# Rounding the quantised tokens and the attention's output on ScalarE in place of VectorE

## The chip, the cores and the metric

The kernel runs on one core of a Trainium2 chip. The metric is the device time of one execution in microseconds (us). The core has TensorE (PE in the profile, PEld for its weight loads), VectorE (DVE), ScalarE (ACT), GpSimd (POOL) and SyncE (SP), which issues the DMAs. Each engine runs its own instructions in order; between engines there are only semaphores.

## The reference, cut to what matters

A block of cross attention and a mixture-of-experts feed-forward; the change lies in the attention alone. There are 8 batches of 512 tokens with 512 channels, 16 heads of 32 channels, and 1601 context rows for each batch.

```python
def _qdq(x):
    s = jnp.maximum(jnp.max(jnp.abs(x), axis=-1, keepdims=True) / 127.0, 1e-08)
    return jnp.clip(jnp.round(x / s), -127.0, 127.0) * s
...
q = _qdq(x) @ _qdq(wq).T + bq            # x is the layer-normed input
kv = cond @ wkv.T + bkv
k, v = jnp.split(kv, 2, axis=-1)
...
attn = jax.nn.softmax(jnp.einsum('bnhd,bmhd->bhnm', q, k) * scale, axis=-1)
o = jnp.einsum('bhnm,bmhd->bnhd', attn, v).reshape(B, N, C)
out = _qdq(o) @ _qdq(wp).T + bp
```

Each `_qdq` of activations rounds to integers. The kernel rounds by adding the constant ROUND = 12582912 to x times 127/max (a float32 of that size has no fraction bits left), and subtracts it again afterwards.

## The kernel before

**Units and slots.** The attention is one long pass over 32 units (8 batches times 4 blocks of four heads). A unit is cut into 28 slots: four heads times 7 groups of key tiles (six groups of 256 keys, one of 65). In a slot `s` PE computes the scores (L493) of slot s into one of two PSUM buffers, ACT takes their exponential (L642) into one of four buffers `a_p`, DVE subtracts the bfloat16 half of it to get the low part `a_p_low` (L764), and PE multiplies both halves with the values (L604) three slots later. Between scores and values PE does a slice of the key and value projections of the next unit (L510, L526). In this text unit 17 is the one that begins at 953.2 us and unit 18 the one from 1002.0 us; "slot 8 of unit 17" counts from the unit's first slot. The pattern of work repeats every four units, a batch.

**The order of everything else.** A class `Plan` puts all other work into slots by tables of numbers (QUANT_SLOTS, OUT_SLOTS, ...). Every engine walks over all slots and, in a slot, first does the exponential (ACT) or the low part (DVE) and then what the plan has there, in the order in which the code lists it. Neither the plan nor its tables are touched by the change.

**The work around the change.** Tokens of a later batch: mean and variance, centring on ACT (L693), the maximum on DVE (L824), scales and the factor `a_q_mul` (L830 to L835), the rounding `q_round` (L838), and three slots later `q_ints` on ACT (L700), which subtracts ROUND, and the transpose on PE. The attention's output of the batch before: POOL normalises it (L905 to L912), DVE takes maxima and the factor `a_o_mul` (L854 to L858), `round` (L861), then `ints` on ACT (L721), transposes, the projection, and on POOL the residual (L950, L956). Each rounding is done four times for a batch, on a tile of 128 tokens by 512 channels, in place. So a batch in the middle of the pass has eight of them: in its second unit `round` in slots 0, 12 and 24 and `q_round` in slots 8 and 20; in its third unit `q_round` in slots 4 and 16 and `round` in slot 8.

**Key and value projections.** Their PSUM results are in banks `ps_p` that ACT reads first (L652, L660: the high parts) and DVE second (L770, L779: the low parts, after which the bank is free). The keys' parts are then stacked by twelve DMAs (L422) into `a_k_stack`, which the scores of the next unit read; the second half of the stack is first needed in slot 5.

```python
for b, m in plan.at("q_round", s):
    dve.tensor_scalar(t["xm"][:, m, :], t["xm"][:, m, :], t["q_mul"][:, m:m + 1], ROUND, ALU.mult,
                      ALU.add).then_inc(q_rounded, 1)
```

## Time and profile before

| | |
|---|---|
| median of 3 runs | 2186.44 us (2184.74 to 2188.13) |
| the profiled execution's own time | 2184.58 us |
| its span, first to last instruction | 2182.8 us |
| busy, share of the span | PE 84%, DVE 82%, ACT 62%, POOL 44% |
| attention's slots | from 135.7 us to about 1690 us |
| granted TensorE clock in them | 0.97 to 1.00 of full speed |

Busy time says how long an engine had an instruction running. The rows further down show, for stretches of one unit, how much of it each engine was busy, who waited for whom, and what stood in a row at some roundings.

### The profile page before, as it was taken

How to read it: one execution, taken by the hardware profiler on the slowest of the kernel's cores; microseconds unless marked ns; L12 is line 12 of the kernel's file. 1: busy time of each engine (PE TensorE's matmuls, PEld its weight loads, DVE VectorE, ACT ScalarE, POOL GpSimd, SP SyncE). 2: the span in 40 equal slices, each digit the busy share in tenths (PEclk: the TensorE clock that was granted, in tenths of full speed). 3: DMA queues.
4: the chain of work that ended last, by engine and by line, in shares of the span. 5: the costliest groups of instructions: out<-in, count | busy, mean ns of one | idle time of the engine just before them, and what ended most of it. 6: DMA issues, size and time to landing. Idle time of an engine off the chain costs nothing. (4 is left out here: it accounts for less than half of the span.)

```text
span 2182.8 us, 60639 instructions
## 1 busy us (share of the span) xinstructions
PE 1822.8 (84%) x24804; PEld 1263.3 (58%) x24804; DVE 1795.8 (82%) x2402; ACT 1346.1 (62%) x1944; POOL 970.5 (44%) x900
## 2 busy tenths in 40 slices
PE   1379998999989998999999898989996216999996
PEld 1247776666666666666666666667774102555553
DVE  4459989899999998999999999989988395666665
ACT  0347876777777777777777777778776332333332
POOL 0002553375256436534733653365334201676765
PEclk7679999999999999999999999999998557999998
DMA  2332331242233223313322332232221244566785
GB/s 87 94 87 51 88 109 34 82 111 80 65 93 104 77 77 92 101 48 89 105 80 65 100 92 75 75 96 78 56 58 32 92 146 138 177 199 220 244 265 169
DMA packets 152823, 225.40 MB, mean 103 GB/s; under 512 B 33861, under 2 KB 87109, under 8 KB 152545
## 3 DMA queue, kind: packets, MB, share of 16 engines
q1 hardware_dynamic: 130736, 166.89, 26.5%
q0 software_dynamic: 21808, 54.58, 8.1%
q8 instruction: 202, 3.31, 0.7%
q14 instruction: 77, 0.62, 0.1%
HBM read 131.37 MB, written 71.32 MB: 93 GB/s over the span
## 5 line engine op out<-in xcount | busy, mean ns | idle before, releaser
L764 DVE TENSOR_TENSOR a_p_low<-a_p 128x1024 f16<-128x1024 f32 (+1 forms) x896 | 1097.2, 1247 | 134.7 <-ACT a_p L642 125.7
L642 ACT ACTIVATE a_p<-ps_s 128x1024 f32<-128x1024 f32 (+1 forms) x896 | 862.1, 967 | 384.9 <-PE ps_s L493 377.5
L493 PE MATMUL ps_s<-a_q_stack,a_k_stack 96*128 96x512 f16 (+1 forms) x1664 | 515.9, 385 | 77.3 <-DMA a_k_stack<-a_k_parts 53.6
L604 PE MATMUL ps_o<-a_v,a_p 128*128 128x65 f16 (+1 forms) x6656 | 447.5, 194 | 19.6 <-ACT a_o_sums L668 9.5
L604 PE MATMUL ps_o<-a_v,a_p_low 128*128 128x65 f16 (+1 forms) x6656 | 447.7, 194 | 0.0
L526 PEld LDWEIGHTS ps_p<-wkv,a_ctx 128*128 128x128 f16 x4992 | 330.4, 99 | 165.7 <-DVE a_v L779 59.2
L526 PE MATMUL ps_p<-wkv,a_ctx 128*128 128x128 f16 x4992 | 379.3, 222 | 44.8 <-DVE a_v L779 44.5
L604 PEld LDWEIGHTS ps_o<-a_v,a_p 128*128 128x128 bf16 (+1 forms) x6656 | 352.1, 98 | 100.3 <-DVE a_p_low L764 24.5
L510 PE MATMUL ps_p<-a_ctx,wkv 128*128 128x384 f16 (+2 forms) x1536 | 349.1, 337 | 37.0 <-DVE a_ctx L402 34.3
L604 PEld LDWEIGHTS ps_o<-a_v,a_p_low 128*128 128x128 f16 (+1 forms) x6656 | 318.1, 98 | 0.0
L510 PEld LDWEIGHTS ps_p<-a_ctx,wkv 128*128 128x128 f16 x1536 | 148.4, 98 | 185.5 <-DVE a_ctx L402 31.0
L905 POOL TENSOR_TENSOR a_o_full<-a_o_sums 128x128 f32<-128x128 f32 x128 | 147.8, 1183 | 202.6 <-ACT a_o_sums L668 202.6
L402 POOL TENSOR_TENSOR a_ctx<-a_ctx_raw,a_ctx 128x384 f16<-128x384 f32 (+2 forms) x112 | 169.2, 1523 | 112.6 <-ACT a_ctx L678 111.9
L1740 PE MATMUL f_ph<-wi_parts,f_xt 128*128 x864 | 200.6, 382 | 4.0 <-DVE f_xt L1807 4.0
L909 POOL TENSOR_TENSOR a_o_full<-a_o_full,o_inv 128x128 f32<-128x128 f32 x128 | 129.6, 1041 | 84.6 <-DVE o_inv L786 83.9
L493 PEld LDWEIGHTS ps_s<-a_q_stack,a_k_stack 96*128 96x128 f16 (+1 forms) x1664 | 114.4, 100 | 83.4 <-issue 77.9
L956 POOL TENSOR_TENSOR a_o_full<-a_o_full,a_x_in 128x512 f32<-128x512 f32 x32 | 88.5, 2767 | 157.9 <-DVE a_o_full L865 157.9
L1681 POOL DMA_INDIRECT f_xs<-d_xr,slots x72 | 81.8, 1136 | 157.6 <-POOLq L48 84.7
L1740 PEld LDWEIGHTS f_ph<-wi_parts,f_xt 128*128 128x128 f16 x864 | 84.7, 98 | 107.9 <-issue 8.3
L1793 ACT ACTIVATE f_gate<-f_ph 128x256 f32<-128x256 f32 x72 | 27.7, 385 | 141.8 <-PE f_ph L1740 141.8
L950 POOL TENSOR_TENSOR a_x_in<-a_x_in,bp_row 128x512 f32<-128x512 f32 x32 | 53.9, 1684 | 132.8 <-DMA a_x_in<-in_x_dram 132.8
L936 POOL TENSOR_SCALAR a_q_nmean<-a_q_mv 128x4 f32<-128x4 f32 x8 | 5.7, 717 | 234.2 <-DVE a_q_rstd L791 234.2
(232 smaller groups left out, 2186.6 us busy)
## 6 DMA issues: line engine op xcount, KB each, us to landing
a_k_stack<-a_k_parts SPq DMA_DIRECT2D x384, 80.0 KB, 2.1
d_ys<-f_y SPq DMA_DIRECT2D x72, 256.0 KB
a_ctx_raw<-in_ctx_dram SPq DMA_DIRECT2D x64, 192.0 KB, 2.5
a_q_stack<-d_q_t SPq DMA_DIRECT2D x96, 128.0 KB, 3.5
a_xm<-in_x_dram SPq DMA_DIRECT2D x8, 1024.0 KB, 5.9
a_ctx_raw<-in_ctx_dram SPq DMA_DIRECT2D x32, 256.0 KB, 4.7
d_q_t<-a_q_parts SPq DMA_DIRECT2D x32, 256.0 KB, 2.7
d_q_full<-a_xm SPq DMA_DIRECT2D x32, 256.0 KB, 2.9
```

Source lines behind the costliest of these rows:

```text
L402: eng.tensor_tensor(t["ctx"][:, 1, c, a:e], t["ctx_raw"][p % NRAW][:, 0:e - a], t["ctx"][:, 0, c, a:e], ALU.subtract).then_inc(ctx_split, 1)
L493: mm = pe.matmul(t["ps_s"][s % 2][0:r, n * N:(n + 1) * N], t["k_stack"][v % 2][0:TERMS * DH, j, kt * P:kt * P + r], t["q_stack"][v % 2][0: ...
L510: mm = pe.matmul(bank(job)[:, 0:e - a], t["wkv"][:, w_part, c, c0:c0 + P], t["ctx"][:, x_part, c, a:e], start=(m == 0), stop=(m == TERMS * ...
L526: mm = pe.matmul(bank(job)[:, n * P:(n + 1) * P], t["ctx"][:, x_part, c, kt * P:(kt + 1) * P], t["wkv"][:, w_part, c, c0:c0 + P], start=(m ...
L604: mm = pe.matmul(t["ps_o"][:, q * VC:(q + 1) * VC], part[0:r, n * N + q * P:n * N + (q + 1) * P], val, start=(g == 0 and n == 0 and low == ...
L642: act.activation(t["p"][s % NP][0:r, 0:len(tiles) * N], t["ps_s"][s % 2][0:r, 0:len(tiles) * N], ACT.Exp, scale=float(DH) ** -0.5 / WSCALE ...
L764: dve.tensor_tensor(t["p_low"][s % NP][0:r, 0:n], full, high, ALU.subtract).then_inc(lows, 1)
L905: last = pool.tensor_tensor(heads[:, j], sums[:, j, :, 0:DH], sums[:, j, :, DH:2 * DH], ALU.add)
L909: last = pool.tensor_tensor(heads[:, j], heads[:, j], t["o_inv"][:, v, j, :, None].to_broadcast([P, QT, DH]), ALU.mult)
L956: pool.tensor_tensor(t["o_full"][b % 2][:, m, :], t["o_full"][b % 2][:, m, :], t["x_in"][i % 2][:, :], ALU.add).then_inc(x2_ready, 1)
L1681: pool.indirect_dma_start(out=xs[n % NX][:, :], out_offset=None, in_=t["xr"][:, :], in_offset=bass.IndirectOffsetOnAxis(ap=t["slots"][:, n ...
L1740: last = pe.matmul(ps_h[n % 2][:, :], xt[n % 2][:, x_part, c, :], t["wi"][:, bass.ds(e, 1), w_part, c, :].rearrange("p a f -> p (a f)"), s ...
```

## The change

Both roundings leave DVE and become activations on ACT: `Identity(scale * x + bias)`, with the factor as scale and a new tile `a_toround`, filled with ROUND, as bias. They stand in the same slots of the plan. In ACT's code `q_round` stands behind centring and ahead of `q_ints`, and `round` behind `q_high` and ahead of `ints`. ACT waits for the factors by `q_scaled`, which was there, and a new semaphore `scaled`. DVE has a wait on the earlier batch's roundings before it overwrites a factor.

```diff
+        scaled = sem("a_scaled")
...
+                for b, m in plan.at("q_round", s):
+                    act.wait_ge(q_scaled, 2 * b + 2)
+                    act.activation(t["xm"][:, m, :], t["xm"][:, m, :], ACT.Identity, bias=t["toround"][:, 0:1],
+                                   scale=t["q_mul"][:, m:m + 1]).then_inc(q_rounded, 1)
...
+                for b, m in plan.at("round", s):
+                    act.wait_ge(scaled, b + 1)
+                    act.activation(t["o_full"][b % 2][:, m, :], t["o_full"][b % 2][:, m, :], ACT.Identity,
+                                   bias=t["toround"][:, 0:1], scale=t["o_mul"][:, m:m + 1]).then_inc(rounded, 1)
...
+            dve.memset(t["toround"][:, :], ROUND)
...
+                    if b >= 1:
+                        dve.wait_ge(q_rounded, b * QT)
                     dve.tensor_tensor(t["q_mul"][:, :], t["tmp"][:, :], t["q_rstd"][:, :], ALU.mult).then_inc(q_scaled, 1)
                     dve.wait_ge(q_scaled, 2 * b + 2)
-                for b, m in plan.at("q_round", s):
-                    dve.tensor_scalar(t["xm"][:, m, :], t["xm"][:, m, :], t["q_mul"][:, m:m + 1], ROUND, ALU.mult,
-                                      ALU.add).then_inc(q_rounded, 1)
...
-                    done(dve.reciprocal(t["o_mul"][:, :], t["so"][:, :]))
-                for b, m in plan.at("round", s):
-                    o = t["o_full"][b % 2][:, m, :]
-                    dve.tensor_scalar(o, o, t["o_mul"][:, m:m + 1], ROUND, ALU.mult, ALU.add).then_inc(rounded, 1)
+                    if b >= 1:
+                        dve.wait_ge(rounded, b * QT)
+                    dve.reciprocal(t["o_mul"][:, :], t["so"][:, :]).then_inc(scaled, 1)
+                    dve.wait_ge(scaled, b + 1)
```

The order of DVE's instructions in unit 17, from the factor `a_q_mul` on (slot 6 to slot 13), before:

```order
L835 TENSOR_TENSOR a_q_mul<-a_tmp,a_q_rstd 128x4
L764 TENSOR_TENSOR a_p_low<-a_p 128x1024 x2
L838 TENSOR_SCALAR a_xm<-a_xm,a_q_mul 128x512
L764 TENSOR_TENSOR a_p_low<-a_p 128x1024
L779 TENSOR_TENSOR a_v<-ps_p,a_v 128x16x32
L764 TENSOR_TENSOR a_p_low<-a_p 128x1024 x2
L865 SCALAR_TENSOR_TENSOR a_o_full<-ps_p,a_so,sp_row 128x512
L764 TENSOR_TENSOR a_p_low<-a_p 128x1024
L770 SCALAR_TENSOR_TENSOR a_k_parts<-ps_p,bk,a_k_parts 128x384
L861 TENSOR_SCALAR a_o_full<-a_o_full,a_o_mul 128x512
L764 TENSOR_TENSOR a_p_low<-a_p 65x512
```

And the same place of DVE in the changed kernel, whose line numbers are some nine higher (L773 is L764, L788 is L779, L779 is L770):

```order
L847 TENSOR_TENSOR a_q_mul<-a_tmp,a_q_rstd 128x4
L773 TENSOR_TENSOR a_p_low<-a_p 128x1024 x3
L788 TENSOR_TENSOR a_v<-ps_p,a_v 128x16x32
L773 TENSOR_TENSOR a_p_low<-a_p 128x1024 x2
L874 SCALAR_TENSOR_TENSOR a_o_full<-ps_p,a_so,sp_row 128x512
L773 TENSOR_TENSOR a_p_low<-a_p 128x1024
L779 SCALAR_TENSOR_TENSOR a_k_parts<-ps_p,bk,a_k_parts 128x384
L773 TENSOR_TENSOR a_p_low<-a_p 65x512
```

The two roundings are gone from between the low parts; nothing else has moved on DVE.

ACT's order at the same place (slot 6 to slot 12 of unit 17), before:

```order
L642 ACTIVATE a_p<-ps_s 65x512
L642 ACTIVATE a_p<-ps_s 128x1024
L729 COPY a_oq_t<-ps_p 128x512
L642 ACTIVATE a_p<-ps_s 128x1024 x2
L660 CAST a_v<-ps_p 128x16x32
L668 COPY a_o_sums<-ps_o 128x260
L642 ACTIVATE a_p<-ps_s 128x1024 x2
L700 ACTIVATE a_xq<-a_xm,a_unround 128x512
L642 ACTIVATE a_p<-ps_s 128x1024
L652 ACTIVATE a_k_parts<-ps_p,bk 128x384
```

And in the changed kernel (L643 is the exponential, L661 and L653 the high parts of values and keys):

```order
L643 ACTIVATE a_p<-ps_s 65x512
L643 ACTIVATE a_p<-ps_s 128x1024
L738 COPY a_oq_t<-ps_p 128x512
L643 ACTIVATE a_p<-ps_s 128x1024
L698 ACTIVATE a_xm<-a_xm,a_toround,a_q_mul 128x512
L643 ACTIVATE a_p<-ps_s 128x1024
L661 CAST a_v<-ps_p 128x16x32
L669 COPY a_o_sums<-ps_o 128x260
L643 ACTIVATE a_p<-ps_s 128x1024 x2
L705 ACTIVATE a_xq<-a_xm,a_unround 128x512
L643 ACTIVATE a_p<-ps_s 128x1024
L653 ACTIVATE a_k_parts<-ps_p,bk 128x384
```

A rounding (L698) now stands between two exponentials, and the later exponentials, high parts and copies are behind it; `round` of slot 12 (L723) follows right behind the last row.

## Rows read from the trace of the kernel before

**Rows 1.** The page: busy times, and VectorE's busy tenths in 40 slices.

```profile
PE 1822.8 (84%) x24804; PEld 1263.3 (58%) x24804; DVE 1795.8 (82%) x2402; ACT 1346.1 (62%) x1944; POOL 970.5 (44%) x900
...
DVE  4459989899999998999999999989988395666665
```

**Rows 2.** Windows of units 17 to 19: length; busy us (instructions) of each engine; clock; DMA.

```profile
953.20:1002.00 48.80, 44.65 (x697) 32.66 (x696) 47.51 (x56) 36.61 (x51) 16.57 (x14) 1.00 0.24 59
1002.00:1052.90 50.90, 45.28 (x701) 32.97 (x700) 46.62 (x46) 38.34 (x57) 28.95 (x19) 1.00 0.33 91
1052.90:1103.50 50.60, 46.35 (x701) 34.00 (x700) 45.20 (x54) 38.84 (x56) 35.76 (x32) 0.97 0.38 110
```

**Rows 3.** Waits in units 16 to 19: us in total, times, longest.

```profile
ACT a_p L642 <- PE ps_s L493: 45.8, 55, 4.7
...
DVE a_p_low L764 <- ACT a_p L642: 13.4, 17, 2.0
...
PE ps_s L493 <- DMA a_k_stack<-a_k_parts: 8.6, 4, 3.4
PE ps_p L526 <- DVE a_v L779: 7.6, 5, 2.4
...
PE ps_s L493 <- ACT a_p L642: 0.3, 1, 0.3
```

**Rows 4.** VectorE's groups by form, units 4 to 30 (311.4 to 1641.5 us).

```profile
L764 DVE TENSOR_TENSOR a_p_low<-a_p 128x1024 f16<-128x1024 f32 x648 | 851.0, 1332 | 101.4 <-ACT a_p L642 95.5
...
L861 DVE TENSOR_SCALAR a_o_full<-a_o_full,a_o_mul 128x512 f32<-128x512 f32 x28 | 30.5, 1091 | 0.0
...
L838 DVE TENSOR_SCALAR a_xm<-a_xm,a_q_mul 128x512 f32<-128x512 f32 x24 | 18.1, 754 | 0.0
```

**Rows 5.** One rounding line alone, same stretch: ns min/median/max.

```profile
L861 DVE TENSOR_SCALAR a_o_full<-a_o_full,a_o_mul x28: 469/1234/1499, 360.6 to 1613.7; 128x512 f32<-128x512 f32 x28
```

**Rows 6.** One of ScalarE's groups by form in the same stretch.

```profile
L742 ACT ACTIVATE a_xn_parts<-a_o_full,a_rstd 128x512 f16<-128x512 f32 x24 | 17.5, 731 | 0.0
```

**Rows 7.** Timeline of VectorE, slots 8 and 9 of unit 17.

```profile
972.66 0.47 DVE L838 TENSOR_SCALAR a_xm<-a_xm,a_q_mul 128x512 f32<-128x512 f32 x1
973.06 1.21 DVE L764 TENSOR_TENSOR a_p_low<-a_p 128x1024 f16<-128x1024 f32 x1
974.19 0.68 DVE L779 TENSOR_TENSOR a_v<-ps_p,a_v 128x512 f16<-128x512 f32 x1
```

**Rows 8.** Timeline of TensorE: the stalls behind rows 7 and rows 9.

```profile
974.93 0.34 PE L526 MATMUL ps_p<-wkv,a_ctx 128*128 128x128 f16 x3 [1.68 <-DVE a_v L779]
```
```profile
1024.55 0.34 PE L526 MATMUL ps_p<-wkv,a_ctx 128*128 128x128 f16 x3 [2.36 <-DVE a_v L779]
```

**Rows 9.** Timeline of VectorE, slots 8 and 9 of unit 18.

```profile
1020.19 1.50 DVE L861 TENSOR_SCALAR a_o_full<-a_o_full,a_o_mul 128x512 f32<-128x512 f32 x1
1021.61 2.28 DVE L764 TENSOR_TENSOR a_p_low<-a_p 128x1024 f16<-128x1024 f32 x1
1023.81 0.68 DVE L779 TENSOR_TENSOR a_v<-ps_p,a_v 128x512 f16<-128x512 f32 x1
```

**Rows 10.** Timeline of GpSimd at the same place.

```profile
1019.14 2.26 POOL L950 TENSOR_TENSOR a_x_in<-a_x_in,bp_row 128x512 f32<-128x512 f32 x1
1021.37 1.44 POOL L956 TENSOR_TENSOR a_o_full<-a_o_full,a_x_in 128x512 f32<-128x512 f32 x1
```

**Rows 11.** Timeline of VectorE, then of ScalarE, slots 20 and 21 of unit 17.

```profile
990.93 0.47 DVE L838 TENSOR_SCALAR a_xm<-a_xm,a_q_mul 128x512 f32<-128x512 f32 x1
991.32 1.21 DVE L764 TENSOR_TENSOR a_p_low<-a_p 128x1024 f16<-128x1024 f32 x1
```
```profile
990.06 1.02 ACT L642 ACTIVATE a_p<-ps_s 128x1024 f32<-128x1024 f32 x1 [0.17 <-PE ps_s L493]
```

**Rows 12.** Timeline of VectorE, slots 24 and 25 of unit 17.

```profile
998.12 1.50 DVE L861 TENSOR_SCALAR a_o_full<-a_o_full,a_o_mul 128x512 f32<-128x512 f32 x1
999.53 1.21 DVE L764 TENSOR_TENSOR a_p_low<-a_p 128x1024 f16<-128x1024 f32 x1
```

More of the change, by code:

```diff
@@ L981, in attention @@
         t["sx_row"], t["unround"] = sb("sx_row", [P, N]), sb("unround", [P, 1])
+        t["toround"] = sb("toround", [P, 1])
         t["st"], t["q_mv"] = sb("st", [P, 2 * QT, 6]), sb("q_mv", [P, QT, 2])
```

## The prediction

> **What bounds the kernel now.** The page comes first. DVE and PE are each busy over four fifths of the span, and in the attention DVE stands at 8 to 9 tenths in nearly every slice [rows 1]. Two engines near full say little until one sees which waits for which, so I next cut one batch into its four units [rows 2]. In unit 17 DVE is busy 47.5 of 48.8 us: nothing is left to take out but DVE's own work. PE is busy 44.7 there and 45.3 of 50.9 in unit 18. So PE stands idle 4.1 us in unit 17 (48.80 − 44.65) and 5.6 in unit 18 (50.90 − 45.28), and ACT 12 in each. Third, the waits of these four units [rows 3]: PE waits 7.6 us in five waits for the values' low part on DVE, and 8.6 us in four waits for the stacked keys, once in each unit; the DMAs of that stack start when DVE has written the keys' low part. PE waits only 0.3 us for ACT's exponential, and ACT 45.8 us for PE's scores. So the pace is set by two queues in turn: PE, while nothing is missing, and DVE at the few places in a unit where a bank or the key stack is late. ACT has spare time and is ahead of DVE at most places, but not at all: DVE waits 13.4 us in 17 waits for it.
>
> **What is removed.** 64 roundings leave DVE: 52 in units 4 to 30 [rows 4], four in units 1 and 2, four before the first slot, four after the last. Their busy time in units 4 to 30 is 30.5 + 18.1 = 48.6 us. That is no gain yet, for two reasons.
>
> First, a rounding alone takes 0.47 us, and 0.40 of queue time, since the next one starts 0.40 after it (973.06 − 972.66) [rows 7]. The rest of the long ones is waiting: L861 goes from 469 to 1499 ns with a median of 1234 [rows 5]. In rows 9 the one at 1020.19 takes 1.50 us while POOL works at L950 until 1021.40 [rows 10]; the low part after it takes 2.28 in place of 1.21 [rows 7, 9] while POOL works at L956. DVE's and POOL's instructions take turns. If the rounding goes, POOL's work is still there, and the next low part meets it instead. So I hold 0.40 of each as surely freed, and the rest as put off to the next low part. The Trainium skill says the same in its own terms (SBUF — State Buffer, section "SBUF: two separate sides": VectorE and GpSimd share a port pair that one of them holds for a whole instruction while the other blocks, also where a VectorE operation has two SBUF inputs); by that rule alone each of the 52 is worth 0.40, 20.8 us in all at most, and the 48.6 us would not come out.
>
> Second, a freed microsecond counts only where PE waits for DVE next. So I go through the eight roundings of a batch:
>
> - Slot 8 of unit 17: two instructions behind the rounding stands the values' low part (L779 at 974.19), for which PE stalls 1.68 us [rows 7, 8]. All of the 0.40 comes out. Gain 0.4 (bounds 0 and 0.4).
> - Slot 8 of unit 18: the same form, stall 2.36 us [rows 8]. The low part at 1021.61 can start up to 1.42 earlier (1021.61 − 1020.19) [rows 9]. It then waits out L950 in the rounding's place, and L956 meets a low part that stands behind L779, when PE has already been released. What is put off is put off past the stall. Gain 1.4 (bounds 0.4 and 1.42).
> - Slot 24 of unit 17: behind it stand a low part and the keys' low part L770, from which the key stack starts [rows 12]. The rounding held 1.41 (999.53 − 998.12), but the exponential now comes later too and POOL's turn stays. I take 0.3, near the low bound (bounds 0 and 1.4).
> - Slots 0 and 12 of unit 17 and slots 4, 16 and 20: slot 0 lies ahead of the unit's wait for the key stack in slot 5, which absorbs it; the others have no PE stall for DVE close behind. At slot 20 I see a loss of lead: the exponential ends at 991.08 (990.06 + 1.02) and DVE wants it at 990.93 [rows 11]; moved back by a rounding it ends near 991.7, and the low part starts 0.4 later than its 991.32 in place of earlier. The five together 0.1 (bounds −0.4, which is slot 20 alone, and 2.0 = 5 × 0.40).
>
> Sum of a batch: 0.4 + 1.4 + 0.3 + 0.1 = 2.2 us. Six batches have all eight roundings: 13.2 us. The four roundings in units 1 and 2 and the four in units 29 and 30 count as half a batch each, 2.2 us together. Sum 15.4 us.
>
> **What is added.** On ACT 64 activations of 128 × 512 with a factor and a bias. The nearest rows are ACT's own of that size, in SBUF, with one such operand: 0.73 us each [rows 6]. No row has both operands as tiles; I take 0.73, with 0.7 and 1.0 as bounds (the upper one is the duration of an exponential on twice the columns [rows 11]). ScalarE: Activation LUTs, section "What ACT_TABLE_LOAD costs", of the Trainium skill has each pointer operand at about 93 ns more; that would be 0.82, and 0.09 × 52 = 5 us of ACT's time. On the path I cost the activations at nothing in the sum: ACT is idle 12 us in each of the two units [rows 2] and gets 5 × 0.65 = 3.3 us (0.73 less the usual overlap of 0.08) in the one and 2.0 in the other. If that cover fails, it is the last rival below. Queued behind a rounding on ACT are the next exponential, the high parts and the copy of the output sums. At slot 8 of unit 17 ACT may also wait for `a_q_mul`, about 1 us, because DVE runs some two slots behind; for the same reason nobody is waiting for the exponentials then. The new waits on DVE (on roundings of the batch before) were met a batch ago: nothing. The memset is one of 128 × 1 ahead of the loop: nothing. The start and the end, eight roundings outside the slots, cost 0.73 in place of 0.47: at most 8 × 0.26 = 2 us if all lie in the chain; against it the last two no longer stand behind other work on DVE. I take nothing.
>
> **The sum.** The profiled execution took 2184.58 us, 1.86 below the median of the runs. 2184.58 − 15.4 = 2169.2; beside the median, 2186.44 − 15.4 = 2171.0. A measurement of this kernel tells 0.2%, or 4.4 us, from no change.
>
> **The rivals.**
>
> *The long roundings' whole time comes out.* For it: over half of them are long [rows 5], and PE's stalls, 4.1 + 5.6 = 9.7 us in two units, have room for it. Against it: the turns with POOL. DVE would lose 48.6 + about 2.6 in units 1 and 2, less 0.08 of overlap for each of 56 and less the seven of slot 4 (some 0.6 each), after which DVE waits anyway: 42.5 us. Time: 2186.4 − 42.5 = 2144; with three quarters of it delivered 2155. Chance 0.12.
>
> *No change that counts.* PE's own work plus the key stack set the pace. For it: PE at 44.7 to 46.4 us in all four units [rows 2], stack waits of 8.6 us in each batch [rows 3] for which twelve DMAs, not DVE, are the long part; what DVE wins it spends waiting for exponentials. Against it: the 7.6 us for L779. Time: 2186 (2182 to 2190). Chance 0.17.
>
> *Slower: the exponentials come late.* A rounding in ACT's queue moves the following exponential by 0.65 us. It decides where ACT's lead over DVE is less than 0.65; from the starts in the trace it is less at slots 20 and 24 of unit 17 and slots 4 and 8 of unit 18, more at the other four. If the lead were gone everywhere, which it may be once DVE has less to do, all 52 would cost 0.65 less the 0.40 freed: +13 us, 2199. The Trainium skill speaks for this side (ScalarE: Activation LUTs, "Rules for kernel authors": adds and multiplies belong on VectorE); the rows agree so far that 0.73 stands against 0.47 [rows 6, 7]. Chance 0.16.
>
> *My forecast*, 0.55: 2171, its own range 2163 to 2182 (the four places at their low bounds give 0.4 us a batch, 2184; with each long one at its full price about 2163).
>
> **How the numbers follow.** Faster: 0.50 of my case and 0.12 of the first rival, 0.62. Within 0.2%: 0.05 and 0.17, 0.22. Slower: 0.16. The range leaves out the far half of the first rival and most of the last: 2155 to 2190.
>
> **What the profile after would show.** DVE's busy time down by 48 to 55 us if its contention goes with the roundings, by 30 if it moves to L764 (now 1332 ns on average for the large form in units 4 to 30). ACT's up by 64 × 0.73 = 47 us. The waits of PE for L779 shorter, above all the one in slot 11 of a batch's third unit (now 2.36 us); PE's waits for ACT still small. Unit 17 near 48.1 and unit 18 near 49.1 us. I am wrong if DVE waits for exponentials by more than it lost in work (then slower), if the low parts do not get longer and the units lose 6 us a batch (then 2150), or if the stack waits grow by what L779's lose (no change).

## The result, and the profile after

The changed kernel took 2149.9 us (median of four runs, 2142.85 to 2151.05) against 2185.59 for the kernel before on the same chip (four runs, 2179.82 to 2188.13): ratio 0.9834, interval 0.9805 to 0.9863, a gain of 36 us. The forecast was 2171, a gain of 15.4; the time lies below the range. The profiled execution took 2150.41 us, 34.2 less than the one of before (2184.58).

The page of the changed kernel, busy times and VectorE's tenths (as [rows 1]):

```profile
PE 1807.6 (84%) x24745; PEld 1258.3 (59%) x24804; DVE 1770.9 (82%) x2339; ACT 1385.7 (64%) x2008; POOL 996.7 (46%) x900
...
DVE  4469989899999899999989999999997395676665
```

DVE is as full as before. Its busy time fell by 24.9 us, where the two lines of the roundings alone held 48.6 in units 4 to 30 [rows 4].

The windows of units 17 to 19 after (as [rows 2]; columns length, PE, PEld, DVE, ACT, POOL, clock, DMA):

```profile
937.00:985.20 48.20, 44.70 (x697) 32.75 (x698) 45.36 (x52) 39.58 (x56) 16.23 (x14) 1.00 0.23 59
985.20:1033.60 48.40, 44.85 (x698) 33.19 (x700) 44.97 (x43) 40.25 (x60) 31.83 (x21) 1.00 0.35 98
1033.60:1080.60 47.00, 44.44 (x699) 32.93 (x700) 44.76 (x54) 38.91 (x56) 40.64 (x30) 1.00 0.39 115
```

Unit 17 is 0.6 us shorter, unit 18 2.5 and unit 19 3.6. Unit 19 has no rounding in it and was in no term of the sum. Its clock rose from 0.97 to 1.00. Keep these two facts.

The waits of units 16 to 19 after (as [rows 3]: us in total, times, longest):

```profile
ACT a_p L643 <- PE ps_s L494: 34.6, 46, 3.1
...
DVE a_p_low L773 <- ACT a_p L643: 11.3, 17, 2.0
...
PE ps_p L527 <- DVE a_v L788: 5.2, 4, 1.9
...
PE ps_s L494 <- DMA a_k_stack<-a_k_parts: 4.9, 4, 1.7
...
PE ps_o L605 <- ACT a_o_sums L669: 2.3, 4, 1.0
```

PE's wait for the values' low part fell from 7.6 to 5.2 us, and that for the stacked keys, to which the prediction gave 0.3 us a batch, from 8.6 to 4.9. DVE doesn't wait longer for exponentials (13.4 and 11.3). PE waits a little longer for ScalarE: 2.3 us for the copies of the output sums, 1.2 before.

**Where the 34.2 us lie.** The first exponential starts at 135.7 us before and at 132.9 after (2.8); the slots take 1544.6 and 1514.3 us (30.2, of which units 4 to 27, the six batches that are alike, 28.4: 1189.9 and 1161.5); what follows, 1.1. I added up PE's idle stretches of over 0.12 us in units 4 to 27 from the records. They are 106.6 us before and 87.4 after: 19.2 of the 28.4. The other 9.2 lie in the time between the stalls, of which 34.1 us are at half of PE's clock before and 17.1 after (below). The places, as means over the six batches (a place is the slot by ScalarE's exponentials; a stall can fall one slot earlier than the slot whose scores wait):

```
place of PE's stall                   before  after
third unit, slot 11 (L779)              2.36   0.95
fourth unit, slot 4 (key stack)         3.07   1.69
third unit, slots 22 and 24 (for DVE)   0.80   0.00
second unit, slot 11 (L779)             1.68   0.99
second unit, slot 4 (key stack)         1.19   0.72
third unit, slot 4 (key stack)          1.77   1.43
third unit, slot 17 (ACT's copy)        0.31   1.01
second unit, slot 3 (DVE's low part)    0.00   0.58
```

### The profile page after: what moved, and what is told of

It is laid out like the page before. It is cut to its first block and busy times, and to the rows that moved or that the text cites. A ratio compares the mean times of both kernels' runs of the same rounds, so it can differ in the third digit from the quotient of the medians.

```text
span 2148.7 us, 60597 instructions
## 1 busy us (share of the span) xinstructions
PE 1807.6 (84%) x24745; PEld 1258.3 (59%) x24804; DVE 1770.9 (82%) x2339; ACT 1385.7 (64%) x2008; POOL 996.7 (46%) x900
## 5 line engine op out<-in xcount | busy, mean ns | idle before, releaser
L773 DVE TENSOR_TENSOR a_p_low<-a_p 128x1024 f16<-128x1024 f32 (+1 forms) x896 | 1120.8, 1274 | 125.7 <-ACT a_p L643 117.5
L643 ACT ACTIVATE a_p<-ps_s 128x1024 f32<-128x1024 f32 (+1 forms) x896 | 861.3, 966 | 309.1 <-PE ps_s L494 303.0
L527 PEld LDWEIGHTS ps_p<-wkv,a_ctx 128*128 128x128 f16 x4992 | 325.3, 98 | 144.9 <-DVE a_v L788 39.8
L527 PE MATMUL ps_p<-wkv,a_ctx 128*128 128x128 f16 x4992 | 373.2, 220 | 28.6 <-DVE a_v L788 28.4
L511 PE MATMUL ps_p<-a_ctx,wkv 128*128 128x384 f16 (+2 forms) x1536 | 346.6, 335 | 34.2 <-DVE a_ctx L403 34.1
L914 POOL TENSOR_TENSOR a_o_full<-a_o_sums 128x128 f32<-128x128 f32 x128 | 157.3, 1257 | 201.7 <-ACT a_o_sums L669 201.7
L403 POOL TENSOR_TENSOR a_ctx<-a_ctx_raw,a_ctx 128x384 f16<-128x384 f32 (+2 forms) x112 | 196.6, 1773 | 83.8 <-ACT a_ctx L679 83.6
L918 POOL TENSOR_TENSOR a_o_full<-a_o_full,o_inv 128x128 f32<-128x128 f32 x128 | 120.5, 970 | 80.8 <-DVE o_inv L795 80.1
L965 POOL TENSOR_TENSOR a_o_full<-a_o_full,a_x_in 128x512 f32<-128x512 f32 x32 | 77.7, 2430 | 132.5 <-DVE a_o_full L874 132.5
```

The costliest lines, as they stand in the source:

```text
L403: eng.tensor_tensor(t["ctx"][:, 1, c, a:e], t["ctx_raw"][p % NRAW][:, 0:e - a], t["ctx"][:, 0, c, a:e], ALU.subtract).then_inc(ctx_split, 1)
L511: mm = pe.matmul(bank(job)[:, 0:e - a], t["wkv"][:, w_part, c, c0:c0 + P], t["ctx"][:, x_part, c, a:e], start=(m == 0), stop=(m == TERMS * ...
L527: mm = pe.matmul(bank(job)[:, n * P:(n + 1) * P], t["ctx"][:, x_part, c, kt * P:(kt + 1) * P], t["wkv"][:, w_part, c, c0:c0 + P], start=(m ...
L643: act.activation(t["p"][s % NP][0:r, 0:len(tiles) * N], t["ps_s"][s % 2][0:r, 0:len(tiles) * N], ACT.Exp, scale=float(DH) ** -0.5 / WSCALE ...
L773: dve.tensor_tensor(t["p_low"][s % NP][0:r, 0:n], full, high, ALU.subtract).then_inc(lows, 1)
L914: last = pool.tensor_tensor(heads[:, j], sums[:, j, :, 0:DH], sums[:, j, :, DH:2 * DH], ALU.add)
```

## The experiments

Ratios are to the kernel before, measured beside each kernel on the same chip, with the 95% interval. On two of the chips the last stage after the attention takes 539 to 554 us in place of about 500, and the kernel before 2230 to 2238 us in all; so I compare ratios, and of the traces only units 4 to 27. All of these kernels have the same plan as before unless the diff says otherwise; each was profiled once. The diffs are cut: "..." and the text say what is left out. What each was for: which roundings carry the gain; whether it is DVE's freed time or another order of turns; what ScalarE's added work costs; and whether the key stack, through the queues behind it, is the second half of the gain.

### Only the tokens, only the outputs, and one of the outputs

Three kernels from the one before. `e1_tokens_only` moves `q_round` alone to ScalarE, `e2_outputs_only` moves `round` alone, and `e3_fourth_output_only` only the `round` of the last 128 tokens, slot 8 of a batch's third unit (e3's lines, first ScalarE's, then VectorE's):

```diff
+                for b, m in plan.at("round", s):
+                    if m < 3:
+                        continue
+                    act.wait_ge(scaled, b + 1)
+                    act.activation(t["o_full"][b % 2][:, m, :], t["o_full"][b % 2][:, m, :], ACT.Identity,
+                                   bias=t["toround"][:, 0:1], scale=t["o_mul"][:, m:m + 1]).then_inc(rounded, 1)
...
                 for b, m in plan.at("round", s):
+                    if m == 3:
+                        continue
...
```

> Only the rounding of the tokens is on ScalarE; the outputs' stays on VectorE. Theory A (a rounding is worth its own 0.40 us of VectorE's queue where TensorE stalls behind it; what it waited for GpSimd moves to the next low part): the stall of 1.7 us in slot 11 of a batch's second unit shrinks to 1.0 to 1.3, that in slot 11 of the third unit stays at 2.4, and the waits for the key stack shrink by under 1 us a batch; 7 to 12 us faster, 2174 to 2179. Theory B (the whole duration comes out, in proportion: 18.1 of 48.6 us): 13 us faster, 2172, and VectorE's low parts do not get longer. If ScalarE's load hurts on its own, no gain.

> Only the rounding of the attention's output is on ScalarE. Theory A: the stall in slot 11 of the third unit goes from 2.4 to 1.0 us, that of the second unit stays at 1.7 or gets shorter by the 0.4 of slot 0 at most, the waits for the key stack shrink by 1 to 2 us a batch; 18 to 26 us faster, 2160 to 2168. Theory B: 30.5 of 48.6 us in proportion, 22 us faster. The two halves together should give the 35.7 us of the change if the effects add; less if they share the same stalls.

> Only one of the eight roundings of a batch moves, the fourth tile of the output, in slot 8 of a batch's third unit, two instructions ahead of the values' low part. Theory A: the stall of 2.4 us in slot 11 of that unit goes to about 1.0, nothing is lost on ScalarE; 1.4 us times 7 is 10 us, 2176, and more only if the key stack's wait in the next unit shrinks too (then up to 17). Theory B: an eighth to a sixth of the change's gain, 5 us, 2181.

Measured: e1 2204.3 us, 0.9883 (0.9866 to 0.9901); e2 2206.92, 0.9906 (0.9889 to 0.9922); e3 2209.02, 0.9912 (0.9885 to 0.9939), with 2229.56 before. e1 gained 25 us where 7 to 12 were expected. By the ratios the two halves make 48 us together, more than the change's 36; by the traces units 4 to 27 are 9.8 us shorter in e1 and 18.1 in e2, together 27.9 where the change has 28.4. Slot 8 of the third unit is what takes slot 11's stall from 2.36 to 0.95: it is 0.96 in e2 and 1.01 in e3, but 2.14 in e1. The stall in slot 4 of the fourth unit goes the other way: 1.30 in e1, 2.76 in e2, 3.12 in e3. So that one is the tokens' doing. The new stall of slot 3 in the second unit is in e2 (0.48) and not in e1, that of slot 17 in the third in e1 (1.01) and not in e2.

### DVE's load given back, ScalarE's doubled

`e8_dve_too` is the changed kernel with a rounding of a tile that nobody needs left on DVE at each of the old places; `e7_act_twice` is the changed kernel with each rounding activation done once more into a tile that nobody reads.

```diff
 e8
+                for _ in plan.at("q_round", s):
...
+                    dve.tensor_scalar(t["dummy"][:, :], t["bv_row"][:, :], t["bv_row"][:, 0:1], ROUND, ALU.mult,
+                                      ALU.add).then_inc(dummied, 1)
...
 e7
+                    act.activation(t["dummy"][:, :], t["xm"][:, m, :], ACT.Identity, bias=t["toround"][:, 0:1],
+                                   scale=t["q_mul"][:, m:m + 1])
...
```

> The changed kernel, with a rounding of idle data into an idle tile put back on VectorE in the places of the old ones (it leaves nothing out and adds 64 operations). VectorE has its old load, ScalarE the new one. If the gain is VectorE's time alone and ScalarE's load is free: 2186, as before. If the late exponentials cost: 2190 to 2199. If the gain came from elsewhere: below 2180.

> The changed kernel with each rounding activation done twice, the first into an idle tile: ScalarE gets another 0.8 us at each of the 64 places. If ScalarE's load is free, as the gain suggests: as the changed kernel, ratio 0.983. If the new waits for the copied sums (slots 3 and 17) grow with it: 0.6 us more at two or three places of a batch, 8 to 13 us slower than the changed kernel, ratio 0.988 to 0.990. Late exponentials everywhere would give 1.00.

Measured: e8 2213.34 us, 0.9927 (0.9909 to 0.9944); e7 2213.43, 0.9911 (0.9892 to 0.9929). With DVE's work given back the stall of slot 11 is 2.36 again, so that part is DVE's time. Yet 0.7% stay, and the fourth unit's stall stays at 1.77. DVE has as many instructions there as before; only their operands and their starts differ. So the load alone doesn't make that part. ScalarE's share is not free: twice the activations take back about half of the gain by the ratios (0.9834 to 0.9911, from different chips), and 6.2 of the 28.4 us by the traces (units 4 to 27: 1161.5 to 1167.7).

### Clearing the queue in front of the key stack, without moving a rounding

The stack's second half is put into SP's queue behind context loads, which wait for a buffer that GpSimd frees, and a store, which waits for GpSimd's addition L956. `e10_before_five_buffers` gives the context loads a fifth buffer; `e12_before_queue_clear` also puts the store four slots later.

```diff
-NRAW = 4
+NRAW = 5
...
-    "gate": dict(logits=1), "project": dict(y=1, x2=2, x2_store=8), "turn": dict(turned=1, project=4),
+    "gate": dict(logits=1), "project": dict(y=1, x2=2, x2_store=12), "turn": dict(turned=1, project=4),
```

> The kernel before with five buffers for raw context instead of four; nothing else. Theory C (the key stack of a batch's fourth unit is late because the queue of SP stands at a context load that waits for a buffer, which GpSimd frees late, since its addition L956 takes 6.66 us there in place of 2.2): the stack's DMAs start right behind the keys' low part, the stall in slot 4 of the fourth unit goes from 3.1 us to 1.2 to 1.7, and the kernel gets 8 to 15 us faster with no work moved at all. If the lateness is VectorE's own, nothing changes.

> The kernel before with five buffers for raw context and the store of the residual sum four slots later, behind the key stack's DMAs in SP's queue. With five buffers alone the queue stood at that store instead, which waits for the same slow addition L956. Theory C: nothing in the queue waits for L956 ahead of the stack now, so the stall of slot 4 in the fourth unit goes from 3.1 to about 1.3 us although L956 still takes 6.66 us; 10 to 20 us faster than before. If the stack is late for another reason: stall near 2.9 and at most 10 us.

Measured: e10 2226.7 us, 0.9954 (0.9935 to 0.9972); e12 2170.8, 0.9929 (0.9903 to 0.9955). From the keys' low part to the stack's first DMA it takes 4.4 us before, 3.05 in e10 and 2.57 in e12, and the stall goes from 3.07 to 2.87 and 2.36. L956 stays at 6.66 us in both. That is far less than the 1.2 to 1.7 and about 1.3 expected, and the shorter stall bought nothing there: units 4 to 27 take 1189.1 and 1188.8 us, against 1189.9 before, with 47.8 and 41.0 us at half clock in place of 34.1. Most of what the two kernels gained lies elsewhere: by their traces 3.5 and 3.3 us before the first exponential and 4.7 and 4.2 in the slots outside units 4 to 27. Nor is the queue clear: in the batch shown further down the stack's DMAs of e12 stand behind a context load that is issued at 1052.70 us, as GpSimd's second conversion ends.

### The stack put earlier

`f1_before_stack_early` puts the stack's last part one slot behind the keys' in place of three, ahead of the loads and the store.

```diff
-                self.put("stack", job[1], job[2] - 2, s + 3)
+                self.put("stack", job[1], job[2] - 2, s + (1 if job[2] == 3 else 3))
```

> The kernel before with the second half of the key stack two slots earlier in SP's order, ahead of the context loads of those slots; what it waits for (the keys' low part) is unchanged. In the kernel before its first DMA starts 4.4 us behind that low part in a batch's fourth unit, with five buffers 3.0, with both queue edits 2.6, and the stall of slot 4 went 3.1, 2.9, 2.4. Theory C: the DMA now starts at once (0.03 us) in all units, the stall is 1.0 to 1.4 us and L956 may stay at 6.66 us; 8 to 14 us faster. If the stall stays above 2.3 although the DMA starts at once, the lateness is elsewhere.

Measured: 2193.21 us against 2187.56, 1.0033 (1.0017 to 1.0049): slower, where 8 to 14 us faster were expected. The stack's first DMA is still 2.57 us behind the keys' low part and not 0.03, again with context loads ahead of it that wait for a conversion on GpSimd. The stall is counted in slot 3 now, with 2.31 us, and ScalarE waits for the context. Its row in the waits of f1, units 4 to 30, then that of the kernel before:

```profile
ACT a_ctx L678 <- DMA a_ctx_raw<-in_ctx_dram: 34.3, 11, 6.1
```
```profile
ACT a_ctx L678 <- DMA a_ctx_raw<-in_ctx_dram: 0.6, 2, 0.4
```

Who stands behind in SP's queue is only exchanged. No run takes the lateness of GpSimd's conversions out of the queue altogether, so how much of the stall they make isn't shown by an edit of the queue.

### Only the first head of the stack waited for

`e5_before_first_head` (and `e6_after_first_head`, the same edit on the changed kernel) lets slot 5 wait for the first head's three DMAs alone, and slot 12 for the other nine.

```diff
                 if s % SLOTS == LATE_GROUP:
-                    pe.wait_ge(keys_in[1][v % 2], 16 * TERMS * HB * (v // 2 + 1))
+                    pe.wait_ge(first_in[v % 2], 16 * TERMS * (v // 2 + 1))
+                if s % SLOTS == GROUPS + LATE_GROUP:
+                    pe.wait_ge(keys_in[1][v % 2], 16 * TERMS * (HB - 1) * (v // 2 + 1))
...
```

> The kernel before; TensorE's wait in slot 5 of a unit is only for the three DMAs of the stack's first head (own semaphore), for the other nine in slot 12. The stalls of slot 4, 1.0 + 1.2 + 1.8 + 3.1 = 7.1 us a batch, mostly go. Theory D (such a wait costs its length, and the clock at the half level behind it on top): 35 to 50 us faster and half-level stretches in the slots down from 34 us. If VectorE is behind by as much anyway, TensorE waits at slot 11 instead and under 15 us come out.

> The changed kernel with the wait in slot 5 cut to the first head's three DMAs. In the kernel before this edit took the waits of slot 4 away (7 us a batch) but gave half of them back at slots 6, 10 and 11 and in half-level clock; 20 us were left. VectorE has less to do here, so less should come back: 20 to 30 us faster than the changed kernel, ratio 0.970 to 0.975. If the same share comes back: 0.975 to 0.98.

Measured: e5 2215.57 us, 0.9909 (0.9889 to 0.9929); e6 2142.39, 0.9791 (0.9762 to 0.982). All stalls of slot 4 are gone in e5, 7.0 us a batch, 42 in units 4 to 27 (0.98 + 1.19 + 1.77 + 3.07), and the kernel gained 20: a miss of the idea that the stack's stall, once gone, comes out whole. Part of it comes back later (slot 6 of the fourth unit 1.80, slot 11 of the third 2.77 in place of 2.36), all stalls together fell by 15.3 only, and PE's time at half clock rose from 34.1 to 58.0 us. Units 4 to 27 are only 5.5 us shorter (1184.4); another 9.0 us lie in the slots outside them.

### The other one of two, and the two together

`g1_fourth_tokens_only` moves only the `q_round` of the last 128 tokens, slot 16 of the third unit; `g2_fourth_of_both` that one and e3's. On ScalarE g2 has e3's lines and these; g1 has these alone, with all outputs on VectorE:

```diff
+                for b, m in plan.at("q_round", s):
+                    if m < 3:
+                        continue
+                    act.wait_ge(q_scaled, 2 * b + 2)
...
```

> Only one of the eight roundings of a batch moves, the tokens' fourth tile in slot 16 of the third unit. No stall on VectorE stands close behind it; my forecast gave it and four others together 0.1 us a batch. Theory C (this rounding keeps VectorE taking turns that GpSimd then lacks, so L956 waits 6.66 us and SP's queue is late): L956 takes 2.8 to 3.9 us, the stall of slot 4 in the fourth unit goes from 3.1 to 1.3 to 1.8, those of slots 22 and 24 go, together 1.8 us a batch; 12 to 18 us faster. By the forecast's pricing: no more than 3 us.

> The two fourth tiles move (slot 8 and slot 16 of the third unit), the other six roundings of a batch stay on VectorE. If these two places carry the change: ratio 0.983 to 0.987, with the stall of slot 11 in the third unit at 1.0 and that of slot 4 in the fourth at 1.3 to 1.8, and without the changed kernel's new stall of 0.6 us in slot 3 of the second unit. If all eight count: 0.988 to 0.992.

Measured: g1 2217.52 us against 2237.8, 0.9908 (0.9883 to 0.9933); g2 2203.63, 0.9847 (0.9821 to 0.9873). Two of the eight roundings of a batch give nearly the whole effect of the change (0.9834, and 26.3 of 28.4 us by the traces): beside these two the six others hardly matter. Without the tokens' they can: e2 is 10.5 us shorter than e3 in units 4 to 27, 2.0 of it in stalls, with 20.5 us less at half clock. In g1 slot 11 keeps its 2.36 and the fourth unit's stall falls to 1.25. By their traces units 4 to 27 take 1182.3 us in e3, 1185.0 in g1 and 1163.6 in g2 (before: 1189.9). The ratios of e3 and g1 say 20 us each, the traces 7.6 and 4.9 there, 3.1 and 4.0 more in the other slots and 1.5 and 0.6 before the first; the profile of before is from another chip, and what the other 8 to 11 us of the ratios are isn't shown.

### The changed kernel again, and versions that go further

`e14_after_again` is the changed kernel once more. `e4_one_step` leaves the rounding pass out altogether: the activation with factor and bias writes float16 with 1536 as the constant (a float16 of that size has no fraction bits left), the transposes are float16, and the copy behind them subtracts 1536 (the last isn't in the cut below). It is meant to give the same integers.

```diff
-                    act.activation(t["xq"][:, :], t["xm"][:, m, :], ACT.Identity,
-                                   bias=t["unround"][:, 0:1]).then_inc(q_ints, 1)
+                    act.activation(t["xq"][:, :], t["xm"][:, m, :], ACT.Identity, bias=t["toround"][:, 0:1],
+                                   scale=t["q_mul"][:, m:m + 1]).then_inc(q_ints, 1)
...
-                ps = bank(job)[:, :].bitcast(BF16)
+                ps = bank(job)[:, :].bitcast(F16)
...
```

`e13_one_step_queue_clear` is e4 with e12's edit, `f2_one_step_stack_early` e4 with f1's, `f3_one_step_first_head` e4 with e5's, `f4_one_step_both` e4 with f1's and e5's.

> The changed kernel itself once more, beside the kernel before, with more rounds and on the chips of the other experiments, whose last stage takes some 540 us in place of 502. If the gain lies in the attention alone: 36 us again, ratio 0.984. The profile should show GpSimd's L965 (L956 before) at 3.92 us in the third unit again, and the same stalls at the same slots.

> The rounding pass goes altogether: ScalarE multiplies, adds 1536 and writes float16, which rounds to an integer, in the place of the operation that subtracted ROUND; the transposes are in float16 and the copies behind them subtract 1536. 64 operations fewer than in either kernel; VectorE as after the change, ScalarE as before it. If VectorE's release makes the gain and ScalarE's load costs the small new waits: ratio 0.975 to 0.981. If the load is free: 0.983.

> The rounding in one step, with the two edits of the queue as well. There L956 takes 3.92 us and the stall is already at 1.35; if it was only the queue, 0 to 0.5 us a batch is left to win: ratio 0.979 to 0.982. If the effects add in full: 0.972.

> The rounding in one step with the same edit. There the first DMA is 1.2 to 3.1 us late and the stall 1.35 us: 0 to 5 us faster than the one-step kernel, ratio 0.977 to 0.981.

> The rounding in one step and the wait of slot 5 cut to the first head's DMAs, two edits that each gained alone (0.981, and 0.4 percent on the changed kernel). If they add: 0.976 to 0.978. If both remove the same stalls: 0.980.

> One step, first head's wait and the stack early. The first head's wait makes the stack's lateness harmless, so nothing over the kernel without the third edit, ratio 0.974 to 0.978; if the stack was also late for slot 12 (stalls at slots 10 and 11), a few us more.

Measured:

```
e14_after_again            2151.67 us  0.9835 (0.9809 to 0.9862)
e4_one_step                2193.02     0.9810 (0.9788 to 0.9832)   long last stage; before 2235.12
e13_one_step_queue_clear   2139.74     0.9781 (0.9754 to 0.9808)
f2_one_step_stack_early    2164.50     0.9895 (0.9876 to 0.9914)
f3_one_step_first_head     2137.35     0.9761 (0.9736 to 0.9785)
f4_one_step_both           2154.43     0.9843 (0.9820 to 0.9866)
```

The change's ratio comes again on another chip; in units 4 to 27 that trace (e14) has the same 87.4 us of stalls as the first, but 23.9 us at half clock in place of 17.1, and 1165.3 us in place of 1161.5. Leaving the pass out is not clearly better than moving it (0.9810 and 0.9834, with overlapping intervals). With the first-head wait it has the lowest ratio of all, 0.9761, ahead of both kernels; e6's and e13's intervals overlap its own. The early stack is worse in every company, against the expectations of f2 and f4.

## Why the prediction was wrong

**Right: slot 8 of the third unit, and where the put-off part goes.** 1.4 us were forecast. The changed kernel at that place, VectorE, GpSimd and TensorE:

```profile
1001.00 3.85 DVE L773 TENSOR_TENSOR a_p_low<-a_p 128x1024 f16<-128x1024 f32 x2
1004.76 0.68 DVE L788 TENSOR_TENSOR a_v<-ps_p,a_v 128x512 f16<-128x512 f32 x1
```
```profile
1001.50 2.25 POOL L959 TENSOR_TENSOR a_x_in<-a_x_in,bp_row 128x512 f32<-128x512 f32 x1
1003.72 2.25 POOL L965 TENSOR_TENSOR a_o_full<-a_o_full,a_x_in 128x512 f32<-128x512 f32 x1
```
```profile
1005.50 0.34 PE L527 MATMUL ps_p<-wkv,a_ctx 128*128 128x128 f16 x3 [0.95 <-DVE a_v L788]
```

The stall is 0.95 where it was 2.36 [rows 8]: 1.41 less, as a mean over the six batches. The two low parts still take turns with GpSimd's two additions (3.85 us for two that take 1.21 each alone [rows 7]). The contention didn't go: it moved to the low parts. Over all slots, the two forms of the low part before, and then after:

```profile
L764 DVE TENSOR_TENSOR a_p_low<-a_p 128x1024 f16<-128x1024 f32 x768 | 1003.4, 1326 | 131.6 <-ACT a_p L642 124.6
L764 DVE TENSOR_TENSOR a_p_low<-a_p 65x512 f16<-65x512 f32 x128 | 98.6, 771 | 3.1 <-ACT a_p L642 1.1
```
```profile
L773 DVE TENSOR_TENSOR a_p_low<-a_p 128x1024 f16<-128x1024 f32 x768 | 1025.2, 1355 | 123.6 <-ACT a_p L643 116.4
L773 DVE TENSOR_TENSOR a_p_low<-a_p 65x512 f16<-65x512 f32 x128 | 100.5, 785 | 2.0 <-ACT a_p L643 1.1
```

They are 23.7 us longer in sum (1125.7 less 1102.0). That is the sign the prediction named for its mechanism (DVE down by about 30 and not by 48 to 55). So the first rival, which had 2144 to 2155, is wrong although its number fits: the long roundings' time did not come out.

**Near its sizes: the other two named places.** Slot 8 of the second unit was 0.4 (bounds 0 and 0.4) and gave 0.69 by its stall (1.68 to 0.99), slightly over the bound; e1 has the same 0.99, e2 has 1.68. Slot 24 of the second unit was 0.3, through the key stack, and the third unit's slot 4 lost 0.34 (0.30 in e2, 0.07 in e1: the outputs' doing). Together the three named terms were 2.1 and measured 2.44.

**The step that failed: "The five together 0.1".** By the stalls a batch lost 3.2 us (19.2 over six), so all other places gave 0.8; but that 0.8 is a sum of large parts of either sign (all gains of a place beside the three named make 3.2, all losses 2.4), and what matters is which part. Slot 16 of the third unit, a `q_round`, had been dismissed because no PE stall for DVE stands close behind. There are two, six and eight slots on (slots 22 and 24, 0.80 us together, gone in the changed kernel). The larger one isn't for DVE, and isn't close: it is the stall for the key stack, sixteen slots on. The prediction had room for it, since the five had 2.0 as their upper bound: its own four upper bounds, 0.4 + 1.42 + 1.4 + 2.0 = 5.22 us a batch, make some 36.5 us and 2150, but its range stopped at 2155. At the other end its four lower bounds make 0.0 us a batch, not the 0.4 it says. That the total meets the sum of the upper bounds is luck: the parts do not. The kernel before, GpSimd, then VectorE, then SP's queue, between the rounding and the stack:

```profile
1042.83 6.66 POOL L956 TENSOR_TENSOR a_o_full<-a_o_full,a_x_in 128x512 f32<-128x512 f32 x1 [2.35 <-DVE a_o_full L865]
1049.45 12.50 POOL L402 TENSOR_TENSOR a_ctx<-a_ctx_raw,a_ctx 128x384 f16<-128x384 f32 x7
```
```profile
1042.68 2.94 DVE L764 TENSOR_TENSOR a_p_low<-a_p 65x512 f16<-65x512 f32 x3
1045.55 0.55 DVE L779 TENSOR_TENSOR a_v<-ps_p,a_v 128x384 f16<-128x384 f32 x1
1046.02 2.34 DVE L764 TENSOR_TENSOR a_p_low<-a_p 128x1024 f16<-128x1024 f32 x2
1048.68 1.90 DVE L764 TENSOR_TENSOR a_p_low<-a_p 128x1024 f16<-128x1024 f32 x1 [0.32 <-ACT a_p L642]
```
```profile
1051.38 3.52 SPq L431 DMA_DIRECT2D a_ctx_raw<-in_ctx_dram  x3
1054.94 0.43 SPq L471 DMA_DIRECT2D d_xr<-a_o_full  x1
1055.41 6.85 SPq L422 DMA_DIRECT2D a_k_stack<-a_k_parts  x11
```

L956 takes 6.66 us; the shortest of its kind takes 1.27. It is ready at 1042.83. DVE then goes through six instructions, the first just begun, none of them prolonged (2.94, 0.55 and 2.34 us), until DVE itself has to wait for an exponential at 1048.36 (0.32 us). Then L956 runs, and is done 1.13 us later. In between, DVE's next low part takes 1.90 in place of 1.21. GpSimd's conversions of the context stand behind it; SP's context load waits for a buffer from them, and the stack's DMAs stand behind the load and the store, so that they start at 1055.41, 2.5 us after the fourth unit has begun (1052.90 [rows 2]); twelve follow each other, and the row has those before the window's end. The changed kernel at the same place, GpSimd and SP:

```profile
1023.06 3.92 POOL L965 TENSOR_TENSOR a_o_full<-a_o_full,a_x_in 128x512 f32<-128x512 f32 x1 [0.49 <-DVE a_o_full L874]
```
```profile
1031.50 1.54 SPq L432 DMA_DIRECT2D a_ctx_raw<-in_ctx_dram  x3
1033.08 0.43 SPq L472 DMA_DIRECT2D d_xr<-a_o_full  x1
1033.55 8.04 SPq L423 DMA_DIRECT2D a_k_stack<-a_k_parts  x12
```

And g1, in which only this rounding has left DVE:

```profile
1037.20 2.78 POOL L971 TENSOR_TENSOR a_o_full<-a_o_full,a_x_in 128x512 f32<-128x512 f32 x1 [0.49 <-DVE a_o_full L880]
```
```profile
1046.94 0.43 SPq L472 DMA_DIRECT2D d_xr<-a_o_full  x1
1047.41 5.08 SPq L423 DMA_DIRECT2D a_k_stack<-a_k_parts  x8
```
```profile
1056.40 0.59 PE L494 MATMUL ps_s<-a_q_stack,a_k_stack 96*128 96x512 f16 x2 [0.30 <-DMA a_k_stack<-a_k_parts]
```

L971 passes in 2.78 us, the stack's DMAs start before the fourth unit's first slot (about 1048.2 by its first exponential), and the stall in this batch is 0.30. The last of the twelve lands 8.1 us after the unit's first exponential in g1 and 11.2 before: 3.1 us, as much as the stalls differ. At the same place the stall is 3.42 before and 1.15 in the changed kernel:

```profile
1064.27 1.01 PE L493 MATMUL ps_s<-a_q_stack,a_k_stack 96*128 96x512 f16 x2 [3.42 <-DMA a_k_stack<-a_k_parts]
```
```profile
1042.97 0.59 PE L494 MATMUL ps_s<-a_q_stack,a_k_stack 96*128 96x512 f16 x2 [1.15 <-DMA a_k_stack<-a_k_parts]
```

Its two ends are shown: g1 and e1 (this rounding alone, and the tokens alone, move the stall), and the stall ends when the last of the stack's DMAs lands. The links between, by which L956 makes the stack late, are read from the traces and argued: e10 and e12 (shorter queue, shorter stall, L956 unchanged) bear them out by 0.2 and 0.7 us of the 3.07 only. In all 20 traces L956 takes 5.5 or 6.66 us at this place where the token rounding of slot 16 is on DVE, and 2.78 or 3.92 where it isn't. Over the six batches this stall is 18.4 us before and 10.1 after. Why GpSimd's addition gets its turn sooner without the rounding stays open: it is ready 0.15 us after a low part has started in both kernels, and e8, which has a rounding on DVE in that place, has the 3.92 us of the changed kernel, though that rounding is one of another tile.

**Missing in the sum: what a stall does to the clock.** The last row of the kernel before shows two matmuls that take 1.01 us together, and 0.59 in the changed kernel. Another batch of the kernel before, TensorE around the same stall (start, us), and windows around it (the clock stands ahead of the last two columns):

```profile
860.63 0.60 PE L493 MATMUL ps_s<-a_q_stack,a_k_stack 96*128 96x512 f16 x2
...
866.33 1.01 PE L493 MATMUL ps_s<-a_q_stack,a_k_stack 96*128 96x512 f16 x2 [3.84 <-DMA a_k_stack<-a_k_parts]
```
```profile
862.90:866.30 3.40, 0.00 (x0) 0.00 (x0) 3.17 (x10) 0.00 (x0) 0.93 (x2) 1.00 0.14 33
866.30:869.70 3.40, 3.37 (x31) 2.60 (x32) 1.26 (x2) 1.95 (x3) 2.74 (x9) 0.51 0.94 281
869.70:873.10 3.40, 3.40 (x58) 2.66 (x57) 1.47 (x3) 2.24 (x4) 2.03 (x6) 0.99 0.19 69
```

PE stood still until 866.3; then the granted clock is at its half level (1.2 in place of 2.4 GHz) until 869.7, and PE gets through 31 matmuls where the next stretch has 58. The kernel before has nine such stretches in units 4 to 27, five of them at this stall of the fourth unit and two at slot 11 of the third; the changed kernel has five. In the 20 profiled executions there are 185, and each begins within 3 us of the end of a PE stall of over 1 us (1.29 at least). Of the stalls from 1 to 2 us 47 of 559 are followed by one, of those from 2 to 3 us 111 of 208, of those over 3 us 27 of 29, of the 792 from 0.3 to 1 us none. And the length of units 4 to 27 less the stalls is 1066.5 us plus 0.46 times the time at half clock (a straight line through the 20, correlation 0.95; the largest miss of it is 4.3 us). That is an estimate from kernels that differ in other things too; the two traces of the changed kernel, with equal stalls, are 3.8 us apart at 6.8 us more of half clock, which fits it. For the change: 0.46 × (34.1 − 17.1) = 7.8 us of the 9.2, and 0.46 × (34.1 − 23.9) = 4.7 with the second trace of the changed kernel. So the clock's share differs from execution to execution, and the kernel before has a single trace. [rows 2] had shown the clock at 0.97 in unit 19, and the prediction quoted PE's 46.35 busy us there as PE's own work; the changed kernel's are 44.44 at full clock. (It also gave PE 44.7 us or more in all four units; rows 2 show three, and in unit 16 PE is busy 43.5.) It goes with e3 and g1 not adding up to g2 in their traces. The stalls nearly add (12.9 and 5.4 us less, 15.6 in g2), but e3 keeps the long stall of the fourth unit and g1 that of slot 11, with 44.4 and 37.5 us at half clock; g2 has neither, and 13.7. It is no full explanation: the kernel before has both long stalls and only 34.1, and what decides which stall is followed by half clock isn't shown.

So the account of the 34.2 us between the two profiled executions: the three named places 2.44 × 6 = 14.6 (forecast 12.6), the rest of the stalls 4.6 (0.6), the clock an estimated 7.8 (none), 1.4 unexplained in units 4 to 27, 1.8 in the slots outside them (2.2), and 3.9 before and after the slots (none; what they come from isn't shown).

**ScalarE's cost: put at nothing on the path, and it was not nothing.** Both rounding groups, units 4 to 30 of the changed kernel:

```profile
L723 ACT ACTIVATE a_o_full<-a_o_full,a_toround,a_o_mul 128x512 f32<-128x512 f32 x28 | 22.7, 812 | 0.0
...
L698 ACT ACTIVATE a_xm<-a_xm,a_toround,a_q_mul 128x512 f32<-128x512 f32 x24 | 19.6, 818 | 8.7 <-DVE a_q_mul L847 8.7
```

They take 0.81 to 0.82 us, not the 0.73 taken from [rows 6]. The Trainium skill's price of a pointer operand, about 93 ns (ScalarE: Activation LUTs, section "What ACT_TABLE_LOAD costs"), had given an estimate of 0.82, and this trace agrees. The wait for `a_q_mul` is 8.7 us in all, about 1.5 each time, where 1 was expected, and covered. Not covered are the small new stalls in slot 3 of the second unit (0.58) and slot 17 of the third (0.31 to 1.01), 1.3 us a batch and 7.7 over the six: a second term that the sum had at nothing, with the other sign. In e4, without the added activations, they are 0.00 and 0.40; in e7, with twice as many, the second is 1.71. The rival with late exponentials had its 13 us only if the lead were gone everywhere; it isn't.

## What to carry to other kernels

An instruction on a busy engine is priced not only by the stall close behind it, but by the turns it leaves to its neighbour on the same memory: follow the neighbour's next slow instruction through what is queued behind it, as far as the next buffer or DMA queue, before calling it free. Price a stall of TensorE at its length and, when it is over 1 us, look whether the matmuls behind it run slower; here that followed about one stall in twelve from 1 to 2 us, half of those from 2 to 3 and nearly all over 3. A long stall taken away alone can give little while another stays (7.6 and 4.9 us alone, 26.3 together), and a stall that an edit shortens can come back elsewhere: compare the length of the whole stretch, not the stall. When a total matches a rival's number, check that rival's own sign (here DVE's busy time) before believing it.

## What the runs showed of the hardware that was not expected

A GpSimd addition of 128 × 512 can wait behind several VectorE instructions in a row: 6.66 us against 1.27 at best, with six VectorE instructions at their undisturbed durations in the meantime. The prediction had the two taking turns one by one. The Trainium skill says that one of the two holds the port pair for a whole instruction (SBUF — State Buffer, "SBUF: two separate sides"); the rows agree with that, and show besides that the waiting one is not always next. The lines of this one instruction in units 4 to 30, before and after (ns min/median/max):

```profile
L956 POOL TENSOR_TENSOR a_o_full<-a_o_full,a_x_in x28: 1271/2184/6657, 381.2 to 1631.6; 128x512 f32<-128x512 f32 x28
```
```profile
L965 POOL TENSOR_TENSOR a_o_full<-a_o_full,a_x_in x28: 2181/2222/3922, 380.0 to 1596.9; 128x512 f32<-128x512 f32 x28
```

A TensorE stall of over 3 us was followed by 3.4 us or more at half clock 27 times of 29, at a price that the line above puts at some 1.6 us each (0.46 × 3.4, an estimate).
